# A graph layer on one core: both halves of a step's edge projection in one place on TensorE, and VectorE's two adds of edge rows in one place

## The reference

```python
def _L0_gnn_ref(x, edge_index, edge_attr, We, be, W1, b1, W2, b2, gamma, beta):
    msg = jax.nn.relu(x[src] + edge_attr @ We + be)
    aggr = jax.ops.segment_sum(msg, dst, num_segments=N)
    z = (1.0 + GINE_EPS) * x + aggr
    h = jax.nn.relu(z @ W1 + b1) @ W2 + b2
    h = jax.nn.relu(h) + x
    ...
def _L0_mix_ref(fx, ...):
    h = linear_no_attn(layernorm(fx, ln1_w, ln1_b), Wx, bx, Wq, Wk, Wv, Wo, bo) + fx
    y = layernorm(h, ln2_w, ln2_b)
    y = jax.nn.gelu(y @ W1.T + b1, approximate=False)
    y = y @ W2.T + b2
    return y + h
...
xn = _layernorm(x, axis=-1)
x = x + _L0_gnn_ref(xn, ...) + _L0_mix_ref(xn[None], ...)[0]
x = x + _L0_ffn_ref(_layernorm(x, axis=-1)[None], ...)[0]
```

## Time and profile before

| | us |
|---|---|
| median of three runs | 3207.47 |
| lowest, highest | 3198.61, 3210.33 |
| the profiled execution's own time | 3208.49 |
| span in the profile, first to last instruction | 3206.8 |
| TensorE busy in matmuls | 2269.7 (71%) |
| GpSimd busy | 1703.9 (53%) |
| VectorE busy | 1504.8 (47%) |
| ScalarE busy | 750.4 (23%) |
| mean granted TensorE clock | 0.841 of full |

### The profile page before, as it was taken

One profiled execution on the slowest core, in us unless ns is written; L12 is line 12 of the kernel. 1 busy time (PEld: TensorE's weight loads), 2 busy tenths in 40 slices (PEclk: granted clock), 3 DMA queues, 4 the chain that ended last, 5 costly groups with the idle time before them and its releaser, 6 DMA issues. The chain is left out here.

```text
span 3206.8 us, 32605 instructions
## 1 busy us (share of the span) xinstructions
PE 2269.7 (71%) x10560; PEld 1460.0 (46%) x10560; DVE 1504.8 (47%) x3056; ACT 750.4 (23%) x1254; POOL 1703.9 (53%) x1689
## 2 busy tenths in 40 slices
PE   2587877888898888877872757677787777736008
PEld 2344655555555555545661434444444444425006
DVE  7696655554555556544761222222222222215893
ACT  1132433333233333322440101111011010101005
POOL 2455655565565556652545656666666666651411
PEclk8698988998999899988975878888878888768559
DMA  6664447443344444332324212221121122111637
GB/s 214 209 172 132 139 119 264 120 118 113 112 122 117 113 119 124 109 97 91 121 70 83 35 32 34 34 40 34 34 40 35 34 40 35 34 26 38 199 102 296
DMA packets 273393, 320.68 MB, mean 100 GB/s; under 512 B 98530, under 2 KB 228023, under 8 KB 272217
## 3 DMA queue, kind: packets, MB, share of 16 engines
q0 software_dynamic: 68416, 133.35, 17.0%
q1 hardware_dynamic: 160280, 144.68, 14.8%
q10 hardware_dynamic: 44544, 40.69, 4.0%
HBM read 241.24 MB, written 77.32 MB: 99 GB/s over the span
## 5 line engine op out<-in xcount | busy, mean ns | idle before, releaser
L747 POOL DMA_INDIRECT c_xg<-xb_dram,src x784 | 777.1, 991 | 577.5 <-PE ps_a L787 260.3
L2171 POOL DMA_INDIRECT er<-row_dram,gi x784 | 742.9, 948 | 433.1 <-issue 431.4
L2226 PE MATMUL ps_em<-zT_all,ew 128*128 128x512 f32 (+1 forms) x832 | 487.2, 717 | 273.4 <-issue 126.5
L2386 DVE TENSOR_TENSOR eo<-ps_en,eb_r 128x1024 f32<-128x1024 f32 (+1 forms) x52 | 60.5, 1163 | 834.6 <-DMA gw<-in_gW 772.6
L2226 PEld LDWEIGHTS ps_em<-zT_all,ew 128*128 128x128 f32 x832 | 183.0, 233 | 550.4 <-issue 391.3
L2291 ACT ACTIVATE hid<-ps_em,eb 128x512 f32<-128x512 f32 (+1 forms) x208 | 133.9, 662 | 1094.2 <-DVE eo L2386 471.9
L2245 PE MATMUL ps_en<-ew,hid 128*128 128x256 f32 x1568 | 348.7, 380 | 0.6 <-DVE deg L2361 0.6
L2245 PEld LDWEIGHTS ps_en<-ew,hid 128*128 128x128 f32 x1568 | 299.8, 191 | 64.8 <-issue 25.8
L774 PE MATMUL ps_e<-c_we,c_eaT 64*128 64x256 f32 x1568 | 235.1, 419 | 49.1 <-DVE c_xg L1104 28.1
L1104 DVE TENSOR_TENSOR c_xg<-ps_e,c_xg 128x1024 f32<-128x1024 f32 x196 | 235.6, 1215 | 19.7 <-DMA c_xg<-xb_dram,src 8.4
L956 ACT ACTIVATE c_xg<-c_xg 128x1024 f32<-128x1024 f32 x196 | 203.7, 1051 | 108.4 <-DVE c_xg L1104 56.7
(11 more groups left out here) (292 smaller groups left out, 2815.8 us busy)
## 6 DMA issues: line engine op xcount, KB each, us to landing
c_eaT<-in_eaT SPq DMA_DIRECT2D x196, 128.0 KB
eo_dram<-eo ACTq DMA_DIRECT2D x48, 512.0 KB
eo<-eo_dram SPq DMA_DIRECT2D x8, 2048.0 KB, 11.1
c_xg<-xb_dram,src POOLq DMA_INDIRECT x784
er<-row_dram,gi POOLq DMA_INDIRECT x784
c_xl<-xn_dram SPq DMA_DIRECT2D x24, 512.0 KB
c_xm<-xm_dram SPq DMA_DIRECT2D x24, 512.0 KB
erow<-c_none ACTq DMA_DIRECT2D x1, 10240.0 KB
```

Source lines behind the costliest of these rows:

```text
L747: pool.indirect_dma_start(xg[:, k % NB, b, :], None, M["xb_dram"], bass.IndirectOffsetOnAxis(ap=M["src1"][:, k * B + b:k * B + b + 1], axi ...
L2171: pool.indirect_dma_start(er[:, r, b, :], None, M["row_dram"], bass.IndirectOffsetOnAxis(ap=gi[:, r, b:b + 1], axis=0)).then_inc(s_get[r], 16)
L2226: m = pe.matmul(ps_m[n % (KE - 1)][:, 0:w], w1[:, e, k, c * P:(c + 1) * P], xT[:, k, at], start=(k == 0), stop=(k == KD - 1))
```

## The change

TensorE issues both halves of the next step's projection at the begin of a step; before, the second half stood between quarters 1 and 2. VectorE issues both adds of edge rows ahead of quarter 3; before, the second stood behind it. No instruction is added or removed, and waits and semaphores are the same.

```diff
--- before.py
+++ after.py
@@ -931,13 +931,12 @@
                     project(0, x)
                 for k in range(S1):
                     if k + 1 < S1:
-                        project(k + 1, 0)
+                        for x in range(2):
+                            project(k + 1, x)
                     units(k, 0)
                     if k:
                         turn_sums(k - 1)
                     units(k, 1)
-                    if k + 1 < S1:
-                        project(k + 1, 1)
                     units(k, 2)
                     add_up(k)
                     units(k, 3)
@@ -1339,10 +1338,9 @@
                     if k:
                         add_window(k - 1)
                     if k + 1 < S1:
-                        add_rows(k + 1, 0)
+                        for x in range(2):
+                            add_rows(k + 1, x)
                     units(k, 3)
-                    if k + 1 < S1:
-                        add_rows(k + 1, 1)
                 add_window(S1 - 1)
                 dve.wait_ge(s_agg, NWIN * S1)
                 dve.wait_ge(s_most, 1)
```

## The result

The changed kernel took 3208.26, 3215.40, 3246.12 and 3246.41 us, median 3230.76; the kernel before, beside it, had a median of 3203.04. The ratio is 1.0101 (95%: 1.0052 to 1.0149). The forecast was 3188, the range ended at 3212. The change makes the kernel about 1% slower. Executions of one kernel on one chip lie up to 2.3% apart; ratios and their intervals leave out those more than 1.5% above the fastest of the same kernel.

A forecast was written before the change was run, and what follows sets the result against it. TensorE was taken to bound the loop from 310 us on. Terms -30 - 6 + 10 + 0 = -26 us, three quarters kept, -20; 3208.5 - 20 - 1.0 gives about 3188 us, range 3168 to 3212.

The forecast's parts named there:

- point 4: TensorE's gaps behind the first half, up to -17 us, and behind the second half's old place, +17 us; counted 0 together.
- Point 3: In front of the joined pair: waiting for VectorE's second add costs 0.28 us in each of 23 + 12 gaps, +10 us.
- point 2: In front of the second half: its six gaps waiting for VectorE's add disappear, -6 us.
- point 6: Gather and load queues: second half's rows needed one quarter of a step earlier, no cost.
- Point 1: TensorE's projection: joining halves saves changes of form, 34.5 us over 97 halves, 30 us without the first 210 us.
- rival of the clock: Granted clock in the loop: one hundredth less is about 10 us; different gaps could take 15 us, 3203; chance 0.10.
- rival of VectorE's pace: At the projection: VectorE paces every pair, all 97 wait, 27 us; gain only 10 us, 3197; chance 0.16.
- Point 5: VectorE's last-quarter units come 1.21 us later: counted 0, bounds no gain and +10 us.
- Three quarters stays: Discount on the summed gain for TensorE's idle time in the loop: of -26 us, three quarters kept, -20 us.
- rival of more cover: Gaps behind the first half close and evictions behind the old place turn out earlier: -34 us, 3173; chance 0.14.
- slower case: Between second and third quarters: without the second half as filler TensorE stalls on evictions; 60 places give +28 us, 3235; chance 0.10.
- signs of a wrong forecast: Loop ending at 1475 us or later, with grown waits on ScalarE or VectorE, or a clock below 0.92.

The follow-up runs named there:

- e6: Changed kernel with TensorE's pair moved between quarters 1 and 2, VectorE's adds joined ahead of quarter 3; 1.0123 of the kernel before, chip 2.
- e2: Kernel before with only VectorE's part of the change, both adds ahead of quarter 3; 1.0026 of the kernel before, chip 1.
- e14: Kernel before with only VectorE's part of the change, both adds ahead of quarter 3, repeated on chip 4; 1.0011 of the kernel before.
- e18: Kernel before, halves still apart, with VectorE's first add ahead of quarter 2 and second ahead of quarter 3; 1.0006 of the kernel before, chip 5.
- e9: Changed kernel with both of VectorE's adds moved ahead of quarter 2; 0.9968 of the kernel before, chip 3.
- e4: Kernel before with both projection halves joined between quarters 1 and 2, VectorE's adds as before; 1.0031 of the kernel before, chip 1.
- e11: Kernel before, halves still apart, with VectorE's first add ahead of quarter 2 and second ahead of quarter 3; 0.9938 of the kernel before, chip 3.
- e12: The kernel of e6 once more, pair between quarters 1 and 2 and adds joined, on chip 3; 1.0038 of the kernel before.
- e1: The changed kernel once more, unaltered, on chip 1; 1.0129 of the kernel before.
- e13: The changed kernel once more, unaltered, on chip 4; 1.0083 of the kernel before.
- e17: The kernel of e9 once more, changed kernel with both adds ahead of quarter 2, on chip 5; 1.0106 of the kernel before.

## Why the prediction was wrong

The step that failed is point 4, which set the cover taken against the cover given and counted 0 for the two; the runs show 41 us more of gaps in quarter 2 against 32 less at the begin of the step. Point 3, a new wait of +10 us, measured +25, comes next to it, and both were hidden by taking TensorE's saved busy time as saved time.

**What held.** A joined pair takes 2.00 us and the next work starts 1.92 after it. The second half's own gaps (point 2) are gone. Nothing came of the queues (point 6), and what follows the loop did not grow.

**Point 1, in the amount.** All of TensorE's busy time in the loop fell by 18 us (mean of three profiles against two), and not by 30. The records of the projection alone are busy 224.9 and 229.3 us before, 198.4 in e6, whose pair never waits, and 211 to 216 in the changed kernel. Between these two stands what the sum left out: a pair right behind a long gap is done at the lower clock, as the one at 830.77. The sum had every pair at 2.4 GHz. For the rest of the difference to 30 there is no row. The rival of the clock adds little to this: over the loop the mean granted clock was 0.926 and 0.922 before and 0.923, 0.919 and 0.913 after, some 6 us at the prediction's own 10 us for one hundredth, and that is part of the busy time above.

**Point 3, the new wait, sized at +10 us and measured at +25.** It took today's gaps, left them as they were, and added 0.28 us each for the slower second add. But a gap is as long as TensorE is early, and the change makes it earlier: from quarter 1's products, with whose eviction VectorE's way to the adds begins, TensorE has 1.26 us less to do until the next pair, since the second half no longer stands between. That this is the reason is argued. Measured is that the gaps grew from 1.2 and 1.5 us on average in the two profiles before to 2.2, 1.7 and 2.0 in the three after. The count was too high as well: six of the 23 + 12 gaps are the second half's own, those of point 2, so 29 first halves were being released by VectorE and not 35. The rival of VectorE's pace made the same mistake and could not get beyond 27 us, and needed all 97 steps for it; the runs have it in fewer than 40.

**Point 4, the cover, taken at 0.** By releaser, the units' waits for ScalarE rose by 29.6 us and the turned sums' fell by 13.1: +16.5. By place, the gaps of quarter 2 rose by 41 us (16.0 to 57.4) and those of quarter 0 and the turned sums fell by 32 (61.2 to 29.3): +9. Both ends were seen and priced at -17 and +17; each is twice as large or more. Taking 0 treated the two as alike. They are not: the half that went to the begin came on top of one that covered part of that wait already, while the place that it left had no other.

**Point 5, VectorE's later units, taken at 0, bound +10.** The units' wait for VectorE rose by 11.2 us on average, but the two profiles before differ by more (18 and 30 us), and the growth is in quarters 1 and 2 (together from 15 to 30 us), not in quarter 3 or at the begin of the next step, where the later units would show. In VectorE's part alone it does not appear (e2 and e14: 22.5 and 20.9 us). So nothing shows this term.

**"Three quarters stays".** The step from 26 to 20 us took a gain in busy time as a gain in time but for a discount. In this loop it does not show as a gain: the sixteen profiles on the slow chips, with TensorE busy 1084 to 1115 us, have loops of 1292 to 1359 us, and the shortest loop of a slow chip (e18) has TensorE busier than 9 of the 11 kernels' profiles with a joined pair. TensorE at 86% was read as the bound; it is one member of a ring with ScalarE and VectorE, which waits for itself. (The rival of more cover, 3173, leaves this discount out, which the others have.)

The slower case was among the rivals, with 0.10, its mechanism being the cover. It had the right sign and the right place, and was held down by the argument that units from 500 us on take 1.8 us and more, longer than their evictions. That argument fails on its own unit: of the 29.6 us more that units wait for ScalarE, 16.5 are in front of L902 (8.5 to 25.0 us on average) and 7.7 in front of L820 (0.7 to 8.5), while L847 and L873 stay as they were (25.5 to 26.3, 14.8 to 13.6). L902's gaps in quarter 2 are also longer than the 1.26 us that the half had covered, 2.8 us each on average. And the rival had only half of the mechanism; the other half is the release.

The signs of a wrong forecast came as listed: the loop ends after 1475 us, with longer waits for ScalarE ahead of quarter 2's units and longer waits of the projection for VectorE, both at once, and in the key/value part a clock of 0.87.

**What stays open.** How much of the 1% is order and how much is the idle stretches of the last section, and whether the order makes these longer; why the pair with early adds is faster than the kernel before on the quick chip (e9) and not on a slow one (e17); and whether joined adds cost anything with the pair in the middle (e4 to e6 on different chips), though alone they cost nothing. On the slow chips single gaps over 3 us, 13 and 14 of them in the two profiles before, are 19 to 27 in all fourteen others, e2 and e18 too, which are not slower; so their count is no explanation.

## What to carry to other kernels

When engines hand work round in a ring, price a move by where it puts each engine's arrival against its releases, and not by the busy time that it saves: a cheaper order that arrives early waits longer, and may then run at the lower clock. A piece of work that splits into two parts, each in front of a different engine's eviction, covers two waits; joined it covers one. Move the release before moving the work that needs it, and measure the two apart: here that alone (e11) was worth 0.6% on one chip and nothing measurable on another.

## What was not expected of the hardware

The same kernel had a median of 2763.63 us on chip 3 and of 3181.72 to 3203.04 elsewhere, with runs within 0.3% of each other there and up to 2.3% apart on one of the others. The gathers are as fast. The page's rows of the changed kernel's profile on a slow chip, then those of e9 on the quick one:

```profile
L2169 POOL DMA_INDIRECT er<-row_dram,gi x784 | 740.8, 945 | 435.9 <-issue 433.8
L2224 PE MATMUL ps_em<-zT_all,ew 128*128 128x512 f32 (+1 forms) x832 | 481.5, 719 | 197.9 <-issue 116.6
```
```profile
PEclk9699999999999999998995999999999975555559
...
L2169 POOL DMA_INDIRECT er<-row_dram,gi x784 | 740.9, 945 | 240.5 <-issue 214.9
L2224 PE MATMUL ps_em<-zT_all,ew 128*128 128x512 f32 (+1 forms) x832 | 352.2, 576 | 24.2 <-DMA eb_r<-in_eb 23.8
```

A gather takes 945 ns on both. The expert products' mean is 719 against 576 ns, and the idle time with no releaser in front of them, 116.6 us, is gone.

In the loop one difference sits in how fast TensorE's results are let go. ScalarE's copy of the window sums by the groups view, 500 to 1475 us, of the kernel before and of e9 (busy, mean ns, idle time before, releasers):

```profile
L951 ACT ACTIVATE c_nsum<-ps_a 128x256 f32<-128x256 f32 x73 | 27.8, 380 | 258.0 <-remote 151.0 <-PE ps_a L787 106.9
```
```profile
L950 ACT ACTIVATE c_nsum<-ps_a 128x256 f32<-128x256 f32 x71 | 27.0, 380 | 210.8 <-PE ps_a L787 210.8
```

On the quick chip each of these waits ends with the last record of TensorE's sums. On the other more than half of the time ends with a release that fits no record. I took the steps in which ScalarE is free when that last record ends. On the quick chip (e9, e11, e12) the copy starts 0.07 us later in all 48. In the two profiles before it does so 0.64 and 0.72 us later in the middle, over 1 us later in 16 and 19 of 43 or 44 steps, and up to 5.1 us later; in the changed kernel's three, over 1 us in 22 or 23 of 45 to 48. From a VectorE add to ScalarE's relu it is 0.03 us on every chip. So on the slow chips TensorE's results are at times released later than its records end, by microseconds. That goes once round the ring: the 5.55 us gap above has 2.7 of it. A plain case is in step 69 of the changed kernel, TensorE's records first, then what waits for them:

```profile
1101.49 1.96 PE L902 MATMUL ps_x<-xn 128*128 128x512 f32 x4 [0.21 <-issue]
1105.42 0.44 PE L796 MATMUL ps_a<-ident,c_nsum 128*128 128x128 f32 x2 [1.98 <-ACT xn L1008]
1105.69 1.88 PE L902 MATMUL ps_x<-xn 128*128 128x512 f32 x4
1115.28 5.46 PE L902 MATMUL ps_x<-xn 128*128 128x512 f32 x6 [7.70 <-ACT xn L1008]
```
```profile
1114.45 0.69 ACT L1008 ACTIVATE xn<-ps_x,c_mb 128x512 f32<-128x512 f32 x1 [8.13 <-remote]
1114.93 0.29 DVE L1116 TENSOR_TENSOR zT_all<-ps_a,zT_all 128x128 f32 x1 [7.77 <-remote]
```

By the records the first unit is done at 1103.45, the turned sums (L796) at 1105.86 and the second unit at 1107.57. ScalarE takes the first unit only at 1114.45 and VectorE the turned sums at 1114.93; TensorE waits for ScalarE, since the third unit needs the first one's tile. From 1107.57 to 1114.45, 6.9 us, none of the three shows any work. The same place costs 8.7, 8.9 and 8.4 us in e1, e13 and e17, and has no gap over 1 us in the two profiles before, in e18 or on chip 3. So the length of these stretches can depend on the order of the program; what happens in them is not in the records.

Without the stretches in which none of the three works, e18's loop is 15 us and e17's 5 us shorter than the mean of the two before. That is the order, and about the size, of the gains of e11 and e9 on chip 3 (19 and 11 us by the medians). It suggests that early adds help on both chips and that on chip 5 the idle stretches hide it, but it rests on single profiles, and the two before differ by 16 us in this figure; it is argued and not shown. The changed kernel itself did not run on chip 3; its nearest relative there, e12, was 0.4% slower than before.
